# Decoder layer on one core: TensorE products reordered and re-banked, VectorE's FFN work reordered

## The reference

```python
# 1. linear attention, no softmax: (q k^T) v, heads of 64
x = layernorm(x + self_attention(x))
# 2. cross attention to 154 context rows, 16 heads of 32, masked softmax
q, k, v = x @ W_q.T + b_q, ctx @ W_k.T + b_k, ctx @ W_v.T + b_v
x = layernorm(x + softmax(where(mask, q k^T / sqrt(32), -1e9)) v @ W_o.T + b_o)
# 3. RWKV channel mix: x_prev is x shifted by one row within a batch
xr = mu_r * x + (1 - mu_r) * x_prev
xk = mu_k * x + (1 - mu_k) * x_prev
x = layernorm(x + sigmoid(xr @ W_r.T) * (square(relu(xk @ W_k.T)) @ W_v.T))
```

## Time and profile before

| | before |
|---|---|
| median of 3 runs | 922.31 us (919.15 to 924.08) |
| the profiled execution | 920.53 us, its span 918.6 us |
| TensorE busy | 885.2 us, 96% of the span |
| VectorE busy | 749.6 us, 82% |
| ScalarE busy | 542.5 us, 59% |
| GpSimd busy | 502.3 us, 55% |
| granted TensorE clock | 0.997 of full speed |

### The profile page before, as it was taken

One profiled execution on the slowest core, in us unless ns is written; L12 is line 12 of the kernel. 1 busy time (PEld: TensorE's weight loads), 2 busy tenths in 40 slices (PEclk: granted clock), 3 DMA queues, 4 the chain that ended last, 5 costly groups with the idle time before them and its releaser, 6 DMA issues.

```text
span 918.6 us, 23123 instructions
## 1 busy us (share of the span) xinstructions
PE 885.2 (96%) x8566; PEld 729.1 (79%) x8566; DVE 749.6 (82%) x2050; ACT 542.5 (59%) x1628; POOL 502.3 (55%) x505
## 2 busy tenths in 40 slices
PE   8999999999899999999999999999999999999997
PEld 7867766888788887878787878787878788878886
DVE  6687566577988889888989898989898889888775
ACT  6556236758565656565756666665656565656631
POOL 1035015667748475757575757575757566656420
PEclk9999999999999999999999999999999999999999
DMA  8792020104313122222322222222222213130001
GB/s 293 242 269 59 26 92 2 43 19 151 100 48 93 55 71 76 65 61 73 120 71 65 79 68 82 66 75 73 71 77 70 77 48 100 48 92 26 1 24 46
DMA packets 82252, 73.80 MB, mean 80 GB/s; under 512 B 7134, under 2 KB 66526, under 8 KB 82014
## 3 DMA queue, kind: packets, MB, share of 16 engines
q1 hardware_dynamic: 78542, 65.27, 23.5%
q10 hardware_dynamic: 3600, 7.08, 2.4%
HBM read 47.73 MB, written 23.33 MB: 77 GB/s over the span
## 4 chain that ended last, share of the span: by engine, by line
PE 33%; DVE 32%; issue 8%; POOL 5%; DMA 5%; SPq 3%; ACT 1%; POOLq 0%; DVEq 0%
PE dense L94 8%; PE dense L95 7%; PE dense L96 7%; DVE mix_k_raw L1293 6%; DVE stats L1176 4%; DVE x_squares L1211 4%; PE turned L1788 4%; DVE prob L1245 3%; DVE x L1220 3%; DMA xt_raw<-x_scratch 2%; SPq L781 2%; PE turned L1810 2%; DVE mix_r_raw L1293 2%; DVE x L1197 2%; PE scores L1774 2%
## 5 line engine op out<-in xcount | busy, mean ns | idle before, releaser
L1545 POOL TENSOR_TENSOR row_inv<-row_sum,minus_one 128x4 f32<-128x4 f32 x128 | 139.7, 1091 | 181.1 <-ACT prob L886 181.1
L886 ACT ACTIVATE prob<-prob,row_min 128x154 f32<-128x154 f32 x512 | 209.7, 417 | 47.6 <-DVE row_min L1245 47.6
L1553 POOL TENSOR_TENSOR weight<-prob,row_inv 128x512 f32<-128x512 f32 x128 | 140.7, 1099 | 0.0
L1245 DVE CUSTOM_DVE_ANT_0 prob<-scores,mask_add 128x154 f32<-128x154 f32 x512 | 127.8, 312 | 4.0 <-PE scores L1774 3.8
L894 ACT ACTIVATE prob_t<-turned 128x512 f32<-128x512 f32 x128 | 75.4, 589 | 48.2 <-PE turned L1788 47.7
L886 ACT ACTIVATION_READ_ACCUMULATOR prob<-prob,row_min 128x1 f32 x512 | 98.6, 193 | 0.0
L94 PE MATMUL dense<-xt_hi,cross_wq_hi 128*128 128x256 f32 x256 | 77.1, 301 | 11.6 <-DVE gate_then_y L1317 11.6
L1788 PE MATMUL turned<-ident,weight 128*128 128x128 f32 x512 | 77.7, 274 | 9.7 <-DVE o_t_lo L1252 8.0
L1788 PEld LDWEIGHTS turned<-ident,weight 128*128 128x128 f32 x512 | 59.9, 140 | 31.9 <-issue 21.3
L94 PE MATMUL dense<-mix_k_hi,ffn_wk_hi 128*128 128x256 f32 x256 | 74.9, 293 | 0.9 <-DVE x L1197 0.9
L95 PE MATMUL dense<-xt_lo,cross_wq_hi 128*128 128x256 f32 x256 | 74.0, 289 | 0.0
(11 more groups left out here) (287 smaller groups left out, 2620.8 us busy)
## 6 DMA issues: line engine op xcount, KB each, us to landing
x_scratch<-x_squares SPq DMA_DIRECT2D x52, 256.0 KB, 2.7
x_rows<-x_rows SPq DMA_DIRECT2D x32, 256.0 KB, 4.4
xt_raw<-x_cols SPq DMA_DIRECT2D x16, 512.0 KB, 3.9
out<-gate_then_y SPq DMA_DIRECT2D x15, 512.0 KB, 3.1
x_t<-x_scratch SPq DMA_DIRECT2D x104, 64.0 KB, 2.1
xt_raw<-x_scratch SPq DMA_DIRECT2D x52, 128.0 KB, 2.8
mask_in<-mask SPq DMA_DIRECT2D x16, 154.0 KB, 2.8
cross_wv<-cross_wv SPq DMA_DIRECT2D x2, 512.0 KB, 6.8
```

Source lines behind the costliest of these rows:

```text
L886: m = act.activation(keys, keys, ACT.Exp, bias=row_min[:, buf, t, h:h + 1], scale=-1.0, accum_out=row_sum[:, buf, t, h:h + 1])
L1245: m = dve.tensor_tensor_reduce(exp_slot(n, u)[:, i * CTX:(i + 1) * CTX], s_bank[:, h, t * CTX:(t + 1) * CTX], mask_add[n % 2][:, t, :], -S ...
L1545: pool.tensor_tensor(row_inv[:, buf, t, :], row_sum[:, buf, t, :], minus_one[:], ALU.pow).then_inc(*p_inv.up)
L1553: pool.tensor_tensor(first, early, inv_early, ALU.mult).then_inc(*p_norm.up)
```

## The change

On **TensorE** the two y products of an iteration move up to stand directly behind the two o products; values(n,0) and scores(n,2) come after them. k(e,1) and r(e,0), r(e,1) move up accordingly, r(e,1) is cut into halves around values(n,1) and scores(n,3), and q(a,0) now stands between transposes(n,2,1) and the first half of v(e,1).

The **banks** change: both halves of q go to d1 and both tiles of v to d0. With that, q(a,0) no longer waits for `v_out` but for the gate of r's second tile (`r_out(n-3, 2)`); o(f,0) no longer waits for `v_out`; k(e,0) waits for `v_out(n-1, 2)`, and v(e,1) for `v_out(n, 1)`.

On **VectorE**: `difference` writes to r's tile, so the blend of k comes first and the blend of r, in place, at the iteration's end. `v_finish(e, 0)` stands ahead of `difference(f)` and `blend(f, "k")`, and both behind `x1_low(a)` and the last `masked_min` of n; `k_mix_low` follows the blend of k directly. `normalise(3, ..)` moves to the next iteration. `turn_x2` is cut in two and placed around `y_finish(a, 1)`; `masked_min(n, 2, ..)` moves behind `normalise_and_turn_x1`.

On **ScalarE**: `mix_high(f, "k")` stands ahead of `take_q(a, 0)`, where `mix_high(f, "r")` stood; the latter moves to the next iteration as `mix_high(e, "r")`. `x_high`, `k_relu_half(e, 1)`, `k_high(e, 1)`, the gates and both `exponentials(n, 3, ..)` are moved. On **GpSimd**, `r_mix_low(e)` stands behind `weigh(n, 1, 1)`, and `scale(1, a)` and `add_bias(a)` ahead of `weigh(n, 2, 0)`. On **SyncE**, the sends of x1 come ahead of both fetches of x2, and the second fetch of x2 comes after that of x1.

No arithmetic is added or removed. The diff, its context lines cut:

```diff
--- before.py
+++ after.py
@@ -653,7 +653,7 @@
...
         mixed, mix = ({g: tile["mix_" + g][part] for g in "kr"} for part in (0, slice(1, 3)))
-        diff_of = lambda n: mixed["r"] if n == 0 else mixed["k"] if n < LAST - 1 else x_in
+        diff_of = lambda n: mixed["r"] if n < LAST - 1 else x_in
         relu, square, ka_hi, ka_lo = tile["k_act"]
@@ -673,7 +673,7 @@
...
         past = {"y": LAST, "q": LAST, "o": LAST - 2, "k": LAST - 3, "r": LAST - 3, "v": LAST - 3}
-        steady = {"y": (d1, d0), "o": (d1, d0), "k": (d0, d1), "r": (d0, d1), "q": (d0, d0), "v": (d0, d1)}
+        steady = {"y": (d1, d0), "o": (d1, d0), "k": (d0, d1), "r": (d0, d1), "q": (d1, d1), "v": (d0, d0)}
         in_loop = lambda kind, n: kind in steady and first_of[kind] <= n <= past[kind]
@@ -805,13 +805,14 @@
...
                     send_x2(f)
-                    fetch_x2(f, 0)
                 if live(a) and moved_x1(a):
...
                 if live(f) and moved_x2(f):
-                    fetch_x2(f, 1)
+                    fetch_x2(f, 0)
                 if live(a) and moved_x1(a):
                     fetch_x1(a)
+                if live(f) and moved_x2(f):
+                    fetch_x2(f, 1)
                 if live(a) and a % GPB == GPB - 1 and a + 1 < NG:
@@ -1019,54 +1020,61 @@
...
                 o_high(f, 3)
+                x_high(a)
                 k_relu_half(e, 0)
...
                 exponentials(n, 1, 0)
-                x_high(a)
                 take_turned(n, 0, 1)
...
                     weight_high("ffn_wr")
+                else:
+                    mix_high(e, "r")
                 o_high(n, 0)
+                k_relu_half(e, 1)
+                take_turned(n, 1, 0)
                 exponentials(n, 2, 0)
-                take_turned(n, 1, 0)
+                k_high(e, 1)
                 take_turned(n, 1, 1)
                 take_rest(n, 1)
-                exponentials(n, 2, 1)
-                k_relu_half(e, 1)
-                o_high(n, 1)
                 if n == 2:
                     weight_high("ffn_wv")
-                k_high(e, 1)
+                exponentials(n, 2, 1)
+                o_high(n, 1)
+                r_gate(e, 0)
+                x1_high(a)
+                r_gate(e, 1)
+                take_turned(n, 2, 0)
                 exponentials(n, 3, 0)
-                r_gate(e, 0)
-                take_turned(n, 2, 0)
-                r_gate(e, 1)
-                x1_high(a)
+                exponentials(n, 3, 1)
                 take_turned(n, 2, 1)
                 take_rest(n, 2)
-                exponentials(n, 3, 1)
-                mix_high(f, "r")
                 if a == GPB - 1:
-                    for k in range(KT):
-                        next_m_high(k)
+                    next_m_high(0)
+                mix_high(f, "k")
                 take_q(a, 0)
                 o_high(n, 2)
-                mix_high(f, "k")
+                if a == GPB - 1:
+                    next_m_high(1)
                 take_turned(n, 3, 0)
...
                 take_q(a, 1)
+                if a == GPB - 1:
+                    next_m_high(2)
                 exponentials(a, 0, 1)
+                if a == GPB - 1:
+                    next_m_high(3)

...
             exponentials(LAST, 1, 0)
+            mix_high(LAST - 2, "r")
             take_turned(LAST, 0, 1)
@@ -1222,11 +1230,10 @@
...

-            def turn_x2(n):
+            def turn_x2(n, t):
                 dve.wait_ge(*o_mm.at(n))
-                for t in range(TPG):
-                    dve.wait_ge(*ln_ok[2].at(n, t + 1))
-                    turn(x2_squares, x2[n % 2], t).then_inc(*tr2_mm.up)
+                dve.wait_ge(*ln_ok[2].at(n, t + 1))
+                turn(x2_squares, x2[n % 2], t).then_inc(*tr2_mm.up)

@@ -1275,7 +1282,7 @@
...
                 elif n:
-                    dve.wait_ge(*k_mm.at(n - 1))
+                    dve.wait_ge(*r_mm.at(n - 1))
                 else:
@@ -1433,49 +1440,52 @@
...
                 k_square(e, 0)
+                if live(e - 1):
+                    normalise(3, e - 1, y3)
                 o_finish(f, 0)
...
                 o_finish(f, 1)
-                o_low(n, 0)
-                masked_min(n, 2, 0)
-                normalise(2, f, x2[f % 2])
-                turn_x2(f)
                 if n == 2:
                     weight_low("ffn_wr")
+                normalise(2, f, x2[f % 2])
                 y_finish(a, 0)
+                turn_x2(f, 0)
+                y_finish(a, 1)
+                o_low(n, 0)
+                turn_x2(f, 1)
+                normalise_and_turn_x1(a)
+                masked_min(n, 2, 0)
+                k_square(e, 1)
                 masked_min(n, 2, 1)
-                y_finish(a, 1)
-                normalise_and_turn_x1(a)
-                k_square(e, 1)
+                k_low(e, 1)
+                if n == 2:
+                    weight_low("ffn_wv")
+                make_mask(a)
                 o_low(n, 1)
                 masked_min(n, 3, 0)
+                x1_low(a)
                 masked_min(n, 3, 1)
-                if n == 2:
-                    weight_low("ffn_wv")
-                k_low(e, 1)
-                make_mask(a)
+                v_finish(e, 0)
                 difference(f)
-                blend(f, "r")
-                x1_low(a)
-                v_finish(e, 0)
                 blend(f, "k")
-                carry(f + 1)
+                k_mix_low(f)
                 o_low(n, 2)
...
                 masked_min(a, 0, 1)
-                k_mix_low(f)
+                v_finish(e, 1)
+                blend(f, "r")
+                carry(f + 1)
                 if a == GPB - 1:
                     next_m_low(0, 1)
-                v_finish(e, 1)
-                normalise(3, e, y3)

...
             masked_min(LAST, 1, 1)
+            normalise(3, LAST - 3, y3)
             for t in range(TPG):
@@ -1609,19 +1619,21 @@
...
                 weigh(n, 1, 1)
+                if e:
+                    r_mix_low(e)
+                scale(1, a)
+                add_bias(a)
                 weigh(n, 2, 0)
-                scale(1, a)
                 weigh(n, 2, 1)
-                add_bias(a)
                 weigh(n, 3, 0)
                 weigh(n, 3, 1)
-                r_mix_low(f)
                 weigh(a, 0, 0)
...

-            for t in range(TPG):
-                weigh(LAST, 1, t)
+            weigh(LAST, 1, 0)
+            r_mix_low(LAST - 2)
+            weigh(LAST, 1, 1)
             scale(2, LAST - 1)
@@ -1755,7 +1767,7 @@
...
                     if h == 0 and n >= 3:
-                        pe.wait_ge(*v_out.at(n - 3, 1))
+                        pe.wait_ge(*r_out.at(n - 3, 2))
                     elif n >= 3:
@@ -1816,8 +1828,6 @@
...
                     pe.wait_ge(*k_sq.at(n - 1, t + 1))
-                elif t == 0 and n >= 2:
-                    pe.wait_ge(*v_out.at(n - 2, 2))
                 elif t == 0 and n:
@@ -1851,7 +1861,7 @@
...
                 elif h == 0 and n <= LAST - 2:
-                    pe.wait_ge(*q_out.at(n + 2, 2))
+                    pe.wait_ge(*v_out.at(n - 1, 2))
                 elif in_loop("k", n):
@@ -1893,8 +1903,10 @@
...
                     pe.wait_ge(*o_sum.at(LAST, t + 1))
+                elif n < LAST - 2 and t == 0:
+                    pe.wait_ge(*r_out.at(n, 1))
                 elif n < LAST - 2:
-                    pe.wait_ge(*r_out.at(n, t + 1))
+                    pe.wait_ge(*v_out.at(n, 1))
                 elif t == 0:
@@ -2000,22 +2012,23 @@
...
                 o_product(f, 1)
+                y_product(a, 0)
+                y_product(a, 1)
                 values(n, 0)
                 scores(n, 2)
-                y_product(a, 0)
+                k_product(e, 1)
                 transposes(n, 1, 0)
-                y_product(a, 1)
+                r_product(e, 0)
                 transposes(n, 1, 1)
-                k_product(e, 1)
+                r_product(e, 1, early)
                 values(n, 1)
                 scores(n, 3)
-                r_product(e, 0)
+                r_product(e, 1, late_half)
                 transposes(n, 2, 0)
-                r_product(e, 1)
+                v_product(e, 0)
                 transposes(n, 2, 1)
-                v_product(e, 0)
+                q_product(a, 0)
                 v_product(e, 1, early)
-                q_product(a, 0)
                 values(n, 2)
```

## The result

The change makes the kernel slower: 957.62 us in the median of five runs (953.75 to 959.51), against 920.33 us for the kernel before (919.15 to 924.08), in five runs beside it. The ratio is 1.0391, its 95% interval 1.0363 to 1.0419. The profiled execution took 953.75 us with a span of 951.8 us, 33.2 us more than that of before. It is the fastest of the five; the others had a granted clock of 0.965 to 0.972 and took 956.5 to 959.5 us.

What follows compares the result with a forecast made beforehand. TensorE's list was taken as the bound. New waits of 40.3 us less 20.5 us of old ones, +19.8 on the profiled 920.53 us, gave 940.3, stated as 940 us, with a range of 919 to 961.

Steps and rivals of the forecast that it cites:

- The new wait: TensorE ahead of scores(a,0) waits for ScalarE's q, some 3 us (costed at 2.9) in each of 13 iterations.
- signs of being wrong: Scores' wait under 1.6 us, another wait taking its place, or the clock showing 0.5 in the loop.
- What is taken away: TensorE's waits in the loop on v's first gate and on o_t_lo, both taken as gone: 20.5 us.
- The floor: Shortest loop iteration without the two kinds of old wait: about 45.7 us.
- X: Time of difference and blend of k on VectorE, beside GpSimd's weighs: taken as 4.6 us.
- X - 1.69: TensorE's wait ahead of scores(a,0): chain of 4.44 + X less 6.13 us of TensorE's own work.
- x1's late arrival: x1 from DRAM, spread 1.4 us; when late, masked_min(n,3,1) delays v_finish: 0.2 us added over the iterations.
- The sum of the waits: All new waits in the loop, 13 x (2.9 + 0.2) = 40.3 us.
- The clock: Rival: TensorE's clock halves at the wait between values and scores; 966 us, 953 if half the iterations; chance 0.20.
- before 160.83 there were also transposes on both sides: Argument against a clock fall in the loop: the earlier fall, ahead of the loop, followed a 2.00 us wait among transposes.
- Values(n,1): Rival: ScalarE's order stalls these products on TensorE, 0.5 to 1.5 us an iteration; 947 to 960 us; chance 0.13.
- the short wait: Rival: the wait ahead of scores(a,0) is short and balances, 1.4 us giving 918 us, or 931 us; not slower 0.17.

Runs made afterwards that it cites:

- mended kernel: Changed kernel with take_q and o_high ahead of mix_high on ScalarE, and k_mix_low behind masked_min(a,0,1) on VectorE: 897.16 us.
- filled kernel: Changed kernel with 20 products of 128x204, results unread, added on TensorE between values(n,2) and scores(a,0): 936.35 us.
- statistics kernel: Changed kernel with the moments of y3's tile 0 moved on VectorE from v_finish(e,0) to behind masked_min(a,0,1): 926.51 us.
- the blend first: Changed kernel with difference(f) and blend(f,k) put back ahead of v_finish(e,0) on VectorE: 915.46 us.
- longer wait: Changed kernel with one more bn_stats, result unread, between v_finish(e,0) and difference on VectorE: 965.03 us.
- held weigh: Changed kernel with both weigh(n,3,..) on GpSimd made to wait until the blend of k has ended: 921.06 us.

## Why the prediction was right, and where its size was off

**The direction and the mechanism** hold. The new wait stands where it was put, between values(n,2) and scores(a,0), behind VectorE's unbroken v_finish, difference and blend and ScalarE's mix_high. An iteration that kept the clock takes 47.95 us, forecast as 48.5 to 49. One of the prediction's own signs of being wrong did appear, the clock at 0.50 in the loop. Undoing either queue's part of it alone removes it there, and mending both gives 897 us.

**What is taken away**: said 20.5 us. The mended kernel's span is 918.6 - 896.6 = 22.0 us under that of before. The floor is 45.3 and not 45.7 us an iteration, which over 13 iterations would be 5.2 us more than said; only 1.5 of them are there. Not all old waits went: of those on o_t_lo one of 1.4 us stays in the loop, in after and in the mended kernel. Where the other 2 us or so went was not followed up.

**The wait's terms.** X was put at 4.6 us, bounds 3.1 and 5.3; it is 4.27 in the mean, 3.92 to 4.53, and 3.02 with GpSimd's weigh steps away. By X - 1.69 the waits would be 2.48 us at X = 4.17 and 2.64 at 4.33; they are 2.60 and 2.77. v_finish was put at 2.29 and is 2.28. x1's late arrival was given 0.2 us in the mean; there are four waits of 3.2 to 3.6 us in place of 2.6, all in the second half, where x1_low and the masked_min behind it end after v(e,0). In these four, ScalarE waited 1.65 to 1.85 us for x1, and up to 1.21 us in the others, and X is 4.52 or 4.53 us. Two of the rows, the first of a quiet iteration:

```profile
297.75 1.06 ACT L869 ACTIVATE xt_hi<-xt_raw 128x1024 fp32r<-128x1024 f32 x1 [0.79 <-DMA xt_raw<-x_scratch]
...
591.08 1.06 ACT L869 ACTIVATE xt_hi<-xt_raw 128x1024 fp32r<-128x1024 f32 x1 [1.65 <-DMA xt_raw<-x_scratch]
```

The sum of the waits was put at 40.3 us and is 37.2. On these alone the span would be 896.6 + 37.2 = 933.8 us.

**The clock** is what was mis-sized. I had it as a rival with a chance of 0.20 and gave the forecast's own value without it. It came true in 8 of 13 iterations, and the 953 us that the prediction gave for half of the iterations is what the profiled execution took. The iteration from 552.87 to 602.94 took 50.07 us; less the floor of 45.30 and the wait of 3.22 at its end, that leaves 1.55 us for a fall of 3.4 us. By the same subtraction the falls of 6.8 us cost 2.5 to 3.2 us each, as a part of such a stretch lies in the wait itself; that is worked out for five of the six, the last having no iteration behind it. Together it is some 19 us, the last taken like the others; the filled kernel gave 18.6. With them the account closes: 896.6 + 37.2 + 19 = 952.8 us against a span of 951.8. The step that failed is the weight against this rival, "before 160.83 there were also transposes on both sides": transposes are no precondition, since values and scores stood beside the wait here, and a wait of 1.62 us was enough in the statistics kernel. I had also taken from the kernel before that waits of up to 1.8 us do no harm; there they did none, but with the blend first a wait of 1.82 us at the same kind of place, between dense products, was followed by a fall. That the time lies in the range is luck in part: with a fall of 2.8 us after every wait the span would be 896.6 + 37.2 + 13 x 2.8 = 970 us (an estimate from these runs), and nothing on record before or since says why it was 8 of 13.

The rule cited for this rival (the Trainium skill, page TensorE: Matmul & The Clock Gate, section "HAM oscillation — how this bites in real kernels"), that a gap recurring in every tile makes the clock fall each time, is nearer to the result than my chance was: 8 of 13 here, 11 of 13 with the longer wait, and not each time.

**Values(n,1)** were put as just in time, with 0.3 us to spare. They are in time: TensorE's waits on prob_t ahead of values come to 1.1 us in the whole span; how much is to spare was not measured. This rival did not happen. Neither did the short wait, and the time of 957.62 us lies in the range of 919 to 961 only by the room left for the clock.

The port rule (the Trainium skill, page SBUF — State Buffer, section "SBUF: two separate sides") agrees with the held weigh for difference and blend, 3.02 us in place of 4.17. That r_mix_low costs nothing beside y_finish and the transposes agrees too: in the mended kernel it ran from 373.45 to 375.83, and beside it a transpose of x2 took 0.69 us and y's sum and statistics 0.65 and 0.69, as elsewhere. A count of inputs is not all of it, though: `normalise`, with one input in SBUF, took 1.39 us at 574.75 in the kernel before, beside a weight step of GpSimd, and 0.51 us at 377.99 in the mended kernel.

## What to carry to other kernels

In a hand-ordered kernel, read each queue for what stands ahead of the operation that the bound engine waits for: here an eviction that had been ready for long stood behind a copy that waited for another engine, which cost 37 us of waits, and moving one entry in each of two queues brought back 60 us in all, with the clock's share. Time a wait on TensorE with its clock: add what the clock does after it, and give it a range, since the same wait did and did not bring a fall here. A price read from the trace includes what another engine did at that moment; before carrying it to a new place, look at which operations of GpSimd will be beside it there.

## What the runs showed of the hardware

- The granted clock fell to 0.5 after waits as short as 1.62 us of TensorE, in 6 of 13 iterations, while other waits of the same length, and two of 2.87 us, left it at 1.00. The same wait of 2.00 us ahead of the loop was followed by a fall in five of ten profiled executions. Length alone does not decide. What else does stays open; that dense products beside the wait help was argued from 2 falls against 6 and not shown.
- A fall can follow a wait between dense products too: one of 1.82 us, one time in 13 waits of 1.0 us in the mean.
- A fall of 3.4 us cost 1.5 us of time, and one of 6.8 us, begun inside the wait, 2.5 to 3.2 us.
- Filling a wait with useless dense products made the kernel 21 us faster, 957.62 to 936.35 us.
- VectorE's difference and blend took 3.02 us with GpSimd held away and 4.16 to 4.53 us in most iterations beside its weigh steps; GpSimd was held as well, its step of 1.01 us (row_inv) taking 1.96 us beside difference.
